# Mamba and mixture-of-experts kernel: the gate projection beside the first scan, one product for B, C and step size, and the last two blocks as routing groups of their own

## The chip, the cores and the metric

One core of a Trainium2 chip runs the whole kernel. The metric is device time in microseconds for one execution, the median of several. The engines run side by side and meet only at semaphores: TensorE (PE) multiplies and transposes, VectorE (DVE) and ScalarE (ACT) do elementwise work and can read TensorE's result banks, GpSimd (POOL) does elementwise work in the main memory of the core and issues indirect DMAs, and SyncE (SP) issues the plain DMAs.

## What is computed

Eight sequences of 1024 tokens with 512 channels pass through two residual layers:

```
n   = layernorm(x)
u,z = n @ in_proj.T                       # 512 and 512 channels
xc  = silu(causal_conv4(u) + conv_b)
B,C,s = xc @ x_proj.T                     # 16, 16 and 1 values for each token
dt  = softplus(s)
h[d,n] = exp(dt*A[d,n]) * h[d,n] + dt*B[n]*xc[d]     # along the tokens
y   = (sum_n h[d,n]*C[n] + D*xc) * silu(z)
x1  = x + y @ out_proj.T
m   = layernorm(x1)
top 2 of 8 experts by m @ router.T + b, weights w1, w2 (normalised)
out = x1 + w1 * (m @ W_e1) + w2 * (m @ W_e2)
```

All of it is in fp32, so each matrix product of the program shows as two matmul instructions.

## The kernel before

The tokens are cut into 16 blocks of 512; two blocks make a sequence. The program is one list of numbered iterations j from -1 to 20 (`iteration`), and each engine walks the same list of steps in the same order and executes those that are its own. Iteration j works on several blocks at once:

- the scan of block j: 64 places (16 states n, four channel groups c). At each place ACT computes a decay (L694) into one of two banks, DVE scans (L817), POOL computes the inputs `u` of two channel groups at a time (L560), PE transposes the states (`h_T`, L997) into one of two banks, and DVE adds them up over the states with weight C (`h_sum`, L829 and L832). `LAG` and `HT` set how many places behind the scan this happens. With LAG = 0 the first of four transposes is issued one place ahead of its sum, the others two places ahead.
- PREP of block j+1: load x, layernorm, transpose, in-projection (`project` 0 to 7, of which 4 to 7 are the gate z), convolution, `silu_x`, `c_project` (B and C by token, 32 matmuls with 32 columns), `dt_project` (8 matmuls with 512 columns), `b_project` (B transposed back), `dt_exp`, `dt_plus`, `b_scale`, `b_store`; the rows of B come back by DMA as `b_ring`. `silu_z` closes the gate.
- POST of block j-1: `y_T`, `y_skip`, `y_gate` (POOL), `out_project`, residual, layernorm, router, top 2, weights, `rank`, and the scatter of the weighted rows to the experts' regions in HBM (two indirect DMAs for each 128 tokens).
- EXPERTS: a routed group (one sequence, 24 tiles of 128 rows) is worked off in two iterations of 12 tiles, two iterations after its post: `rows_load`, four transposes, an eviction, 8 matmuls, an eviction and a store. `new_sequence` computes the group's table on DVE in odd iterations; it waits until the stores of the tiles before are done.
- COMBINE of block j-5: `fetch` of x1, two accumulating indirect gathers for each 128 tokens, `store`.

Where a side step stands among the 64 places is written out by hand in tables (`POST`, `PREP`, `EXPERTS`, `COMBINE`). Side work takes one of four result banks (`WORK`). A step that waits blocks everything behind it on its engine, and SP's loads and stores are such steps as well.

Scans run in iterations 0 to 15. Iteration 16 has the last four sums, the post of block 15 and 12 tiles; 17 and 18 have 12 tiles each (`closing_steps`, with two buffers for the rows), and combine goes on until iteration 20. At the start all weights are loaded on SP's queue ahead of x (L428 to L436), and every engine waits for all of them before its first step.

## Time and profile before

| | |
|---|---|
| median of 3 runs | 3035.31 us (3031.69 to 3042.91) |
| profiled execution, its time | 3033.59 us |
| its span, first to last instruction | 3031.7 us |
| PE busy | 2435.8 us, 80% |
| DVE busy | 2314.1 us, 76% |
| ACT busy | 1435.6 us, 47% |
| POOL busy | 1810.3 us, 60% |
| mean granted clock of TensorE | 0.887 of full speed |

### The profile page before, as it was taken

The page shows a single profiled execution, that of the slowest core. Times are in us where ns is not written, and L with a number is a line of the kernel's source. Part 1 is how long each engine was busy: PE and PEld are TensorE (multiplying, and loading weights), DVE is VectorE, ACT ScalarE, POOL GpSimd, SP SyncE. Part 2 cuts the span into 40 slices and gives each one's busy share as a digit, 9 for nine tenths or more (in the row PEclk, how much of TensorE's full clock was granted, in tenths as well). Part 3 has the DMA queues.
Part 4 walks back from the last instruction along what each step waited for, and adds up shares of the span by engine and source line. Part 5 has one row for each costly group of instructions (what it writes and reads, how often), then busy time and mean ns, then how long its engine had stood idle before and what let it go on. Part 6 is the DMA issues. An engine that isn't in the chain of part 4 may idle for free.

```text
span 3031.7 us, 35667 instructions
## 1 busy us (share of the span) xinstructions
PE 2435.8 (80%) x10000; PEld 1466.7 (48%) x10000; DVE 2314.1 (76%) x3233; ACT 1435.6 (47%) x2386; POOL 1810.3 (60%) x1418
## 2 busy tenths in 40 slices
PE   5677777798979899798979898797979898778770
PEld 3344444454545555455545554554545454544330
DVE  1788998988888888888888887888888888881000
ACT  2453546354555546354545546464545555342220
POOL 0555666556566757567676767577666767572223
PEclk9777777799989999898979999899989899888895
DMA  1773432223234434334334444344334444343665
GB/s 58 260 253 102 140 125 80 87 81 114 77 102 115 129 112 129 108 115 132 108 112 119 126 122 131 110 117 131 107 114 121 129 115 126 105 144 110 175 173 109
DMA packets 195502, 373.16 MB, mean 123 GB/s; under 512 B 23024, under 2 KB 23024, under 8 KB 195312
## 3 DMA queue, kind: packets, MB, share of 16 engines
q1 hardware_dynamic: 146576, 263.91, 27.1%
q0 software_dynamic: 28672, 67.13, 10.5%
q10 hardware_dynamic: 20064, 39.85, 3.6%
q8 instruction: 87, 1.43, 0.2%
q14 instruction: 103, 0.84, 0.1%
HBM read 212.99 MB, written 157.81 MB: 122 GB/s over the span
## 4 chain that ended last, share of the span: by engine, by line
PE 38%; DVE 19%; issue 16%; POOL 11%; ACT 9%; DMA 5%; SPq 1%; DVEq 0%; POOLq 0%; ACTq 0%
PE work L992 28%; DVE h L817 7%; POOL u L560 6%; PE hT L997 6%; DVE acc L832 6%; ACT decay L694 2%; DVE xc L850 2%; PE work L997 2%; DMA x_out<-result_scratch,rows_of 2%; POOL x_out L661 1%; PE work L1046 1%; ACT L694 1%; POOL row_scratch L645 1%; POOL row_scratch L647 1%; ACT xc L730 1%
## 5 line engine op out<-in xcount | busy, mean ns | idle before, releaser
L560 POOL TENSOR_TENSOR u<-xc,b_ring 128x1024 f32<-128x1024 f32 x512 | 1230.8, 2416 | 778.8 <-DVE h L817 424.2
L694 ACT ACTIVATE decay<-dt,neg_a 128x512 f32<-128x512 f32 x1024 | 699.7, 689 | 680.4 <-DVE h L817 671.3
L997 PE MATMUL hT<-ident,h 128*128 128x128 f32 x4096 | 680.7, 305 | 320.9 <-DVE acc L832 173.4
L997 PEld LDWEIGHTS hT<-ident,h 128*128 128x128 f32 x4096 | 530.4, 157 | 573.6 <-DVE acc L832 246.9
L832 DVE SCALAR_TENSOR_TENSOR acc<-hT,ct,acc 128x512 f32<-128x512 f32 x960 | 700.2, 730 | 134.1 <-PE hT L997 132.5
L992 PE MATMUL work<-w_exp,xeT 128*128 x1536 | 721.1, 614 | 34.1 <-ACT xeT L784 15.5
L817 DVE TENSOR_TENSOR_SCAN h<-decay,h_last,u 128x512 f32<-128x512 f32 x512 | 653.0, 1275 | 90.7 <-ACT decay L694 66.7
L817 DVE TENSOR_TENSOR_SCAN h<-decay,u 128x512 f32<-128x512 f32 x512 | 621.5, 1214 | 106.6 <-ACT decay L694 92.3
L992 PE MATMUL work<-xnT,w_in 128*128 128x512 f32 x1024 | 469.2, 602 | 0.8 <-ACT xnT L709 0.8
L992 PEld LDWEIGHTS work<-w_exp,xeT 128*128 128x128 f32 x1536 | 286.7, 195 | 361.8 <-issue 360.5
L661 POOL DMA_INDIRECT x_out<-result_scratch,rows_of x128 | 205.8, 1608 | 189.6 <-DMA x_out<-x_scratch 100.2
L992 PEld LDWEIGHTS work<-xnT,w_in 128*128 128x128 f32 x1024 | 188.4, 194 | 192.9 <-issue 192.9
L992 PE MATMUL work<-w_out,sz 128*128 128x512 f32 x512 | 256.1, 648 | 4.7 <-POOL sz L582 4.7
L792 ACT ACTIVATE ye<-work 128x512 f32<-128x512 f32 x180 | 106.0, 589 | 241.2 <-PE work L992 223.0
L784 ACT ACTIVATE xeT<-work 128x512 f32<-128x512 f32 x192 | 112.7, 588 | 130.6 <-PE work L997 127.4
L992 PEld LDWEIGHTS work<-w_out,sz 128*128 128x128 f32 x512 | 103.1, 212 | 114.0 <-issue 114.0
L850 DVE SCALAR_TENSOR_TENSOR xc<-work,w_conv,xc 128x511 f32<-128x511 f32 (+2 forms) x192 | 142.2, 741 | 17.7 <-ACT edge L717 16.3
L997 PE MATMUL work<-ident,xe 128*128 128x128 f32 x720 | 112.0, 279 | 41.2 <-DMA xe<-row_scratch 41.1
L582 POOL TENSOR_TENSOR sz<-xc,sz 128x512 f32<-128x512 f32 x64 | 79.8, 1269 | 85.8 <-DVEq L876 85.8
L997 PEld LDWEIGHTS work<-ident,xe 128*128 128x128 f32 x720 | 86.4, 145 | 55.1 <-issue 54.8
L702 ACT ACTIVATE xn<-xn,shift,rstd 128x512 f32<-128x512 f32 x64 | 51.3, 807 | 120.2 <-POOL shift L550 120.2
L992 PE MATMUL work<-w_xp,xc 128*128 128x32 f32 x512 | 74.2, 305 | 23.9 <-ACT xc L730 23.9
(140 smaller groups left out, 1892.5 us busy)
## 6 DMA issues: line engine op xcount, KB each, us to landing
b_ring<-b_scratch SPq DMA_DIRECT2D x256, 256.0 KB, 3.9
xe<-row_scratch SPq DMA_DIRECT2D x180, 256.0 KB
result_scratch<-ye SPq DMA_DIRECT2D x180, 256.0 KB
row_scratch<-x_out ACTq DMA_DIRECT2D x32, 1024.0 KB, 5.0
xn<-in_x SPq DMA_DIRECT2D x64, 256.0 KB, 4.6
x<-in_x SPq DMA_DIRECT2D x64, 256.0 KB, 4.3
x_scratch<-x SPq DMA_DIRECT2D x64, 256.0 KB, 4.4
x_out<-x_scratch SPq DMA_DIRECT2D x64, 256.0 KB, 3.3
```

The source lines that it names most:

```text
L560: nc.gpsimd.tensor_tensor(out=u[:, at:at + 2, :], in0=xc[:, half, 2 * k:2 * k + 2, :], in1=b_ring[:, n % ROWS:n % ROWS + 1, :].to_broadcas ...
L582: nc.gpsimd.tensor_tensor(out=sz[:, 1 - half, c, :], in0=xc[:, 1 - half, c, :], in1=sz[:, 1 - half, c, :], op=ALU.mult).then_inc(y_gated, 1)
L661: nc.gpsimd.indirect_dma_start(x_out[:, q % 2, :], None, res_dram[:, :], bass.IndirectOffsetOnAxis(ap=rows_of[(pair - 3 + half) % 3][:, at ...
L694: nc.scalar.activation(decay_bank[g % 2][:], dt[:, half, :], ACT.Exp, scale=neg_a[:, c, n:n + 1]).then_inc(decay_ready, 1)
L702: nc.scalar.activation(xn[:, q % 2, :], xn[:, q % 2, :], ACT.Identity, bias=shift1[:, q:q + 1], scale=rstd[:, q:q + 1]).then_inc(xn_ready, 1)
L784: nc.scalar.activation(xeT[:, i % 2], ps[:].rearrange("p (k t) -> p k t", k=C), ACT.Copy).then_inc(free, 1)
L792: nc.scalar.activation(ye_of(j, i), ps[:], ACT.Copy).then_inc(free, 1)
L817: nc.vector.tensor_tensor_scan(out=h[:, n % 2, c, :], data0=decay_bank[g % 2][:], data1=u[:, g % UR, :], initial=first, op0=ALU.mult, op1= ...
L832: nc.vector.scalar_tensor_tensor(out=acc[:, q, :], in0=hT_bank[k % HT][:], scalar=ct[:, ip, q, m:m + 1], in1=acc[:, q, :], op0=ALU.mult, o ...
L850: nc.vector.scalar_tensor_tensor(out=xc[:, 1 - half, c, away:T], in0=ps[:, 0:T - away], scalar=w_conv[:, c, EDGE - away:TAPS - away], in1= ...
L992: last = nc.tensor.matmul(ps, left(k), right(k), start=(k == 0), stop=(k == C - 1))
L997: last = nc.tensor.transpose(ps[:, k * P:(k + 1) * P], tile(k), ident[:])
```

## The change

- **Start.** SP loads the four x tiles of block 0 first (the third and fourth into `x1`), then the first half of `w_in`, then the rest; seven small weights are issued by ACT. Each engine waits only for what its next step needs.
- **Gate.** `project` 4 to 7 become `z_project`. In every iteration from 0 on they stay in the same iteration; those of block 0 move from iteration -1 into the first places of iteration 0, with their evictions and `silu_z`.
- **B, C and step size.** One `xp_project` (8 matmuls with 512 columns, 33 rows of result) takes the place of `c_project`; `xp_evict` (ACT) copies its 33 rows into `dt`; `dt_project` becomes 2 matmuls that pick the row of the step size and spread it over 128 rows; `c_T` transposes C (4 transposes), with one eviction; B is scaled straight from the result bank.
- **Lag.** LAG is 1: sums and transposes run one place later, and every transpose is issued two places ahead of its sum.
- **Groups.** Blocks 0 to 13 make seven groups of two with 23 tiles each; blocks 14 and 15 are groups of their own with 15 tiles each. Tiles of a group run as 12 and 11 in iterations 3 to 14; the seventh group's 23 all run in iteration 15; the two last groups' 15 in iterations 16 and 17. Combine takes two blocks in iteration 15 and two in 16, one in 17 and one in 18; the last block is gathered into `x1`, whose x1 rows are fetched ahead. From iteration 15 on the tiles alternate between two buffers. The table of a group (`new_group`) has two copies. Zeroing of the result buffer is gone.
- All places in the tables are new.

```diff
-    XT = TOP * SQ + E
-    LAG = 0
+    GROUPS = [(b, 2) for b in range(0, BLOCKS - 2, 2)] + [(BLOCKS - 2, 1), (BLOCKS - 1, 1)]
+    TILES = [TOP * Q * n + E - 1 for first, n in GROUPS]
+    for g in range(len(GROUPS) - 3):
+        EXPERT_PLAN[2 * g + 3] = (g, 0, XT - XT // 2)
+        EXPERT_PLAN[2 * g + 4] = (g, XT - XT // 2, XT // 2)
+    for i in range(3):
+        g = len(GROUPS) - 3 + i
+        EXPERT_PLAN[BLOCKS - 1 + i] = (g, 0, TILES[g])
+    COMBINE_PLAN = {j: [j - 5] for j in range(5, BLOCKS - 1)}
+    COMBINE_PLAN[BLOCKS - 1] = [BLOCKS - 6, BLOCKS - 5]
+    COMBINE_PLAN[BLOCKS] = [BLOCKS - 4, BLOCKS - 3]
+    COMBINE_PLAN[BLOCKS + 1] = [BLOCKS - 2]
+    COMBINE_PLAN[BLOCKS + 2] = [BLOCKS - 1]
+    LAG = 1
...
-        "c_project": [34.97, 38.72],
-        "dt_project": [40.54],
-        "dt_exp": [44.54],
-        "b_project": [44.57],
-        "b_store": [55.2],
+        "dt_project": [38.23],
+        "dt_exp": [41.7],
+        "xp_project": [37.25],
+        "xp_evict": [40.85],
+        "c_T": [40.72],
+        "b_store": [45.82],
...
+    FIRST_GATE = [(0.2 + 2 * c, ("z_project", c, 0)) for c in range(C)] + [(1.6 + 2 * c, ("z_evict", c, 0)) for c in range(C)] + [(9, ("silu_z", 0, 0))]
...
+        if j == BLOCKS + 2:
+            return ([("gather", q, 0) for q in range(Q)] + [("gather", q, 1) for q in range(Q)] + [("store", q) for q in range(Q)])
...
+        rows = [[("fetch", q), ("gather", q, 0), ("gather", q, 1), ("store", q)] for q in range(Q)] + [[("fetch_last", q) for q in range(Q)]]
+        steps = [("new_group", 0)]
+        for i, tile in enumerate(tiles):
+            steps += tile
+            steps += rows[i // 3] if i % 3 == 0 and i // 3 < len(rows) else []
...
+            for q in range(Q):
+                sync.dma_start(xn_of(0, q), x[q * P:(q + 1) * P, :]).then_inc(first_loaded[q], 16)
+            sync.dma_start(w_in[:, :, 0:D], in_w[:, 0:D].rearrange("(k p) n -> p k n", p=P)).then_inc(project_loaded, 16)
+            sync.dma_start(w_in[:, :, D:2 * D], in_w[:, D:2 * D].rearrange("(k p) n -> p k n", p=P)).then_inc(weights_loaded, 16)
...
+                    elif s[0] == "xp_evict":
+                        bank_no, before = use_of(j, ("xp_project", 0))
+                        act.wait_ge(work_full[bank_no], before + 1)
+                        nc.scalar.activation(dt[0:XP, 1 - half, :], work_bank[bank_no][0:XP, :], ACT.Copy).then_inc(xp_ready, 1)
...
+                        product(ps[0:XP, :], lambda k: w_xp[:, k, :], lambda k: xc[:, 1 - half, k, :]).then_inc(full, 1)
                     elif s[0] == "dt_project":
                         ps, full = take(j, s)
-                        pe.wait_ge(xc_ready, (p + 1) * C)
-                        product(ps[:], lambda k: w_xp[:, k, 2 * N:2 * N + 1].to_broadcast([P, P]),
-                                lambda k: xc[:, 1 - half, k, :]).then_inc(full, 1)
+                        pe.wait_ge(xp_ready, p + 1)
+                        nc.tensor.matmul(ps[:], pick_dt[0:XP, :], dt[0:XP, 1 - half, :], start=True, stop=True).then_inc(full, 1)
```

## Rows read from the trace of the kernel before

**Rows 1.** The span in 40 slices: busy tenths of DVE, and TensorE's granted clock.
```profile
DVE  1788998988888888888888887888888888881000
PEclk9777777799989999898979999899989899888895
```

**Rows 2.** Stages: us; busy PE, PEld, DVE, ACT, POOL; clock; DMA; GB/s.
```profile
86.50:227.30 140.80, 95.00 (x368) 62.58 (x369) 124.96 (x147) 68.99 (x115) 77.24 (x45) 0.71 0.75 261
227.30:385.30 158.00, 116.86 (x481) 76.76 (x480) 143.72 (x193) 77.66 (x121) 99.47 (x78) 0.77 0.37 123
...
1554.20:1725.70 171.50, 147.12 (x624) 88.33 (x624) 148.66 (x211) 88.44 (x144) 112.86 (x85) 0.92 0.40 117
1725.70:1891.10 165.40, 146.31 (x626) 88.59 (x626) 140.57 (x194) 89.79 (x156) 113.73 (x90) 0.94 0.42 122
...
2563.50:2718.10 154.60, 116.56 (x487) 73.62 (x488) 135.35 (x189) 64.35 (x103) 105.34 (x76) 0.84 0.41 120
2718.10:2838.60 120.50, 86.80 (x269) 43.33 (x268) 20.83 (x66) 24.56 (x42) 34.61 (x45) 0.87 0.45 129
2838.60:2889.80 51.20, 49.91 (x144) 23.89 (x144) 0.00 (x0) 12.90 (x24) 10.85 (x8) 0.95 0.70 184
2889.80:2954.30 64.50, 50.02 (x144) 24.16 (x144) 0.00 (x0) 13.69 (x25) 13.73 (x9) 0.91 0.66 171
2954.30:3031.70 77.40, 0.00 (x0) 0.00 (x0) 0.00 (x0) 0.00 (x0) 24.59 (x16) 0.50 0.54 112
```

**Rows 3.** Timeline, first 87 us: start, duration, engine, line, operation, idle before.
```profile
9.06 13.78 SPq L447 DMA_DIRECT2D xn<-in_x  x4
...
15.84 0.69 DVE L837 BATCH_NORM_STATS2 stat<-xn 128x6 f32<-128x512 f32 x1 [14.44 <-DMA xn<-in_x]
...
31.79 17.01 PE L992 MATMUL work<-xnT,w_in 128*128 128x512 f32 x32 [0.78 <-ACT xnT L709]
...
53.52 7.03 PE L992 MATMUL work<-w_xp,xc 128*128 128x32 f32 x32 [4.71 <-ACT xc L730]
...
60.36 6.09 PE L992 MATMUL work<-xc,w_xp 128*128 128x512 f32 x8
...
66.49 0.60 ACT L737 ACTIVATE sp<-work 128x512 f32<-128x512 f32 x1 [5.62 <-PE work L992]
...
74.50 0.34 SPq L461 DMA_DIRECT2D b_scratch<-sp  x1
...
79.62 4.65 POOL L560 TENSOR_TENSOR u<-xc,b_ring 128x1024 f32<-128x1024 f32 x2 [51.48 <-DMA b_ring<-b_scratch]
...
86.51 4.57 DVE L817 TENSOR_TENSOR_SCAN h<-decay,u 128x512 f32<-128x512 f32 x4 [12.04 <-ACT decay L694]
```

**Rows 4.** Timeline, iteration 10 at `c_project`: start, duration, engine, line, operation, idle before.
```profile
1833.58 1.87 PE L992 MATMUL work<-w_xp,xc 128*128 128x32 f32 x16
...
1837.26 3.60 PE L992 MATMUL work<-xc,w_xp 128*128 128x512 f32 x8
```

**Rows 5.** Groups by line, whole span: count | busy, mean ns | idle before.
```profile
L832 DVE SCALAR_TENSOR_TENSOR acc<-hT,ct,acc 128x512 f32<-128x512 f32 x960 | 700.2, 730 | 134.1 <-PE hT L997 132.5
```

**Rows 6.** Timeline, the end: start, duration, engine, line, operation, idle before.
```profile
2832.26 0.35 DVE L959 TENSOR_TENSOR table_row<-tiles_to,tile_no 1x192 f32<-1x192 f32 x1 [43.52 <-DMA result_scratch<-ye]
...
3002.27 1.54 POOL L661 DMA_INDIRECT x_out<-result_scratch,rows_of  x1 [0.30 <-issue]
...
3007.59 1.54 POOL L661 DMA_INDIRECT x_out<-result_scratch,rows_of  x1 [3.79 <-DMA x_out<-result_scratch,rows_of]
...
3012.65 0.34 SPq L503 DMA_DIRECT2D out<-x_out  x1
...
3016.40 0.32 SPq L498 DMA_DIRECT2D x_out<-x_scratch  x1
3019.23 1.54 POOL L661 DMA_INDIRECT x_out<-result_scratch,rows_of  x1 [1.71 <-DMA x_out<-x_scratch]
...
3024.30 1.54 POOL L661 DMA_INDIRECT x_out<-result_scratch,rows_of  x1 [3.54 <-DMA x_out<-result_scratch,rows_of]
```

613 lines of the change are left out of this document (337 added, 276 removed).

## The prediction, made before the changed kernel ran

> **What bounds the kernel now.** I read the span in slices first [rows 1]: DVE is busy 80 to 90% of each slice for nine tenths of the span, idle in the first slice but for a tenth, and idle again in the last three. So there are three stages: a start, a long loop, and an end. Then I cut the span at the first scan of each iteration [rows 2]. The first scan starts at 86.5 us. A full iteration takes 165.4 us (even j) or 171.5 us (odd j, with the table of a group); DVE is busy 140.6 to 148.7 us of it, 85 to 87%, PE 146 to 147 us, 86 to 88%. Two engines are near full together, and the 23 to 25 us in which DVE is idle are mutual waits of in-order queues. The last scan ends at 2718.1 us, and 313.6 us follow that hold 21 us of DVE work: 120.5 us with post of block 15 and 12 tiles, then 24 tiles, then 77.4 us in which PE does nothing and only gathers run. The clock is 0.92 to 0.94 in the full loop and 0.71 to 0.77 in its first two iterations.
>
> Of the waits in the loop, I read the groups by line [rows 5]: DVE waits 134.1 us before `h_sum` for transposes, 8.4 us an iteration. Going through the instances of the twelve full iterations, about half of it, 4.0 us, stands before the first of each four sums: the one that the schedule gives a lead of one place only.
>
> **The change part by part.** The sum is made against the profiled execution, 3033.6 us, which is 1.7 us under the median of the runs shown.
>
> *Start.* x is issued at 9.06 us behind 3 MB of weights and DVE's first statistics begin at 15.84; the second pair comes later still, and the first product starts at 31.79 [rows 3]. With x ahead of all, the first statistics can start at about 5.2 us (issue at 0.7, and some 4.5 us to land, the median of x loads in the list of DMA issues). The chain from there to the second eviction took 7.3 us, and a second pair that no longer waits adds some 3.5 us: first product at 16 us, 15.8 us earlier. The first half of `w_in` is there by then: 3.1 MB landed in 14.3 us, so x and that half, 2 MB, need some 9 us. ACT's seven DMA issues take the 7 us that SP needed for them and end at about 8 us, ahead of its first `norm_apply`.
> The Trainium skill, "DMA: Bandwidth & Descriptors", section "Issuing engines are not separate DMA queues", says that DMAs issued from several engines interleave on the same 16 DMA engines and save only issue time. By that rule the small weights and `w_out` could hold the first half of `w_in` back until all 4.2 MB are there, and the sum would be worse by up to 3 us. No run here shows it yet.
>
> Behind the convolution nothing changes until `silu_x` ends at 53.5. Then `c_project` takes 7.03 us and `dt_project` 6.09, so `dt_exp` starts 13.0 us later, at 66.49 [rows 3]. New: 8 matmuls (3.4 us, or 6.8 at half clock), a copy of 0.6, two matmuls (0.9 to 1.7) and some 0.5 of semaphores, 5.4 to 9.6 us; I take 7.5, a gain of 5.5. From `dt_exp` to `b_store` it is 8.0 us before, because B's transposes stand behind 16 gate matmuls; without that 6.0. From `b_store` to the end of the first `u` it is 7.5 us and stays so, but the first scan began at 86.51 only, 4.5 us after that `u`, since ACT was still at `silu_z`; that goes. In all the first scan comes 28 us earlier (20 to 30).
>
> *The gate of block 0* now lies beside the first scan: 32 matmuls, 13.8 us at full clock and 27 at half, four evictions and a `silu_z` of 4.5 us with its table loads. Half of the matmuls can run in the gap of some 13 us in which DVE waits for B to come back; the rest stands between the transposes of an iteration whose clock is 0.71 [rows 2]. DVE pays 8 us (2 to 18).
>
> *The loop, B, C and step size.* At full clock 16 matmuls of `c_project` take 1.97 or 1.87 us and the 8 of `dt_project` 3.60 [rows 4]. Removed: 3.8 + 3.6 us. Added: 3.6 for `xp_project`, 0.9 for two matmuls, and transposes for transposes. PE has 2.9 us less. ACT swaps four copies of 0.19 us for one of 0.6 and one of 0.2. The added wait: `dt_project` at place 38 waits for `xp_evict` at place 40 on ACT, and `h_T` is queued behind it on PE. ACT gets there after the decay of place 40, which needs scan 38. From the end of scan 38 that is 0.7 + 0.6 us, the two matmuls 0.9, and the transposes 0.7 with 0.5 for semaphores, 3.4 us; DVE has three scans and two sums to do before it needs them, 5.5 us. So the lag covers it; under LAG = 0 it would cost some. I take it as nothing, and 2 us an iteration if the cover is gone.
>
> *Lag.* Every transpose gets two places of lead, 3.7 us, so the 4.0 us before the first sums go. What is late next is the product that stands ahead of a transpose (3.6 us), and that remains. At the border of two iterations `y_T` now waits for a sum that is one place later, and its 16 transposes stand ahead of the next sum: +1.2 us.
> Together with 1.5 us for the shorter PE queue I take -4.3 us in each of twelve full iterations, -52 us. The bounds are wide, since every place in the tables is new: -90 (all of the 8.4 us of waits for transposes goes, net of the border) and +15.
>
> *Iteration 15* gets 11 tiles more. A tile is 4.16 us of PE (49.91 us for 12 tiles, rows 2, third row from the end), so PE goes from 116.6 to 162.4 us. At the share that full iterations reach (88%) that is 183 us, with PE alone as the bound 165; I take 180, as DVE has 5 to 13 us less to do there than in a full iteration. Against 154.6: +25 us (8 to 40). The eight added gathers cost POOL 13 us, hidden if first and second gather of a pair have a `u` between them.
>
> *Iteration 16* has 15 tiles instead of 12 and combines two blocks. Before, it took 120.5 us to the first transposes of the next stage, the last part of it because the table waited 43.5 us for the last store (released at 2832.26) [rows 6]; the two copies end that. Now POOL is late: a block's gathers in the free-running end take 38.7 us (77.4 for two), so 77 for two, 22 for its other work (34.6 less 8 gathers of 1.6) and 14 until the first: 113, and SP's last store behind it. I take 122, +2 us (-12 to +20).
>
> *Iteration 17.* Before, 24 tiles from 2838.6 to the last product at 2949.6, 111 us. Now 15 tiles. In `closing_steps` SP has `fetch`, then `store` of the same rows right behind it, and waits there for both gathers: 2.8 us from fetch to gather, 5.3 to the second and 5.1 to the store [rows 6], 13.2 us in which neither a load nor a store of a tile is issued. Three more loads, of which one must land, and the third store take some 5 us, so 18.5 us for three tiles instead of 12.5. Four such groups and three tiles more make 86.5 us: -24.5 us. If SP didn't hold the tiles it would be 62, so -49.
>
> *After the last product*: 82 us before (block 14 and 15 one after the other). Now eight gathers that don't wait on each other, 1.84 us apart, 12.9 us to the last; 0.8 and 2.5 before them for eviction and store, then 5.1 and 2.3 to the end as in the last rows: 24, with some reserve 26. -56 us.
>
> Sum: -28 + 8 - 52 + 25 + 2 - 24.5 - 56 = -125.5. 3033.6 - 125.5 = 2908, and 2910 for the median.
>
> **The rivals.**
> - *The loop gains nothing.* The new places and the waits for `xp_evict` eat what the lag gives. For it: the tables are a whole, 8.4 us of waits are only a third of DVE's idle time, and most of the rest is ACT's (decays behind `silu_x`, `dt_exp` and `silu_z`), which isn't touched. Loop 0 to +10 us: 2965.
> - *The loop gains twice as much*, or SP doesn't hold the tiles in iteration 17: 2860 to 2885. For it: in iterations with fewer products the same DVE work runs with less idle time (158.0 us with 143.7 busy).
> - *The tiles moved forward cost what they save.* Iteration 15 at 195 us and iteration 16 at 140, bound by POOL, whose gathers stand ahead of `rank` weights and scatters: +33 us, 2943.
> - *Slower: the clock falls.* PE's work is 88% of an iteration at clock 0.93; with 117 us of work in 155 to 158 us the rows show 0.77 and 0.84 [rows 2]. Less work, in shorter pieces, could bring the lower level (1.2 GHz) back into the loop. Outside the full iterations the sum is -73.5 us, so they would have to be 6.1 us longer, 174.5 instead of 168.4 on average. At 88% that is PE at 153.6 us with 144 us of today's work: the clock falls below 0.93 x 144 / 153.6 = 0.87. At 0.84, the value of iteration 15, it would be 159 us of work, 181 us an iteration, +152 us: 3112. Against it: full iterations have a quarter more PE work than those, and lose 2%.
> - *The change doesn't do what it says* at the end: the table or the scatters hold iteration 17 anyway. That is within the 140 us of the third rival.
>
> **How the numbers follow.** Forecast 0.50, loop without gain 0.18, loop with twice the gain or a free SP queue 0.15, moved tiles costly 0.12, clock 0.05. A measurement of this kernel can tell about 0.5%, 15 us, from no change. Within it lies part of the second case with a bad end (0.02), above it nearly all of the clock's case (0.03), so 0.95 faster, 0.02 same, 0.03 slower. The range leaves out the clock's case and the outer parts of the bounds: the uncertain terms (loop +-35, iteration 15 +-15, 16 +-16, 17 +-20, gate +-8) combine to some 45 us. 2855 to 2975.
>
> **What would show it.** Right: first scan near 58 us; full iterations at 161 to 167 us with the idle time of `h_sum` at half; iteration 15 near 180; about 86 us of tiles in iteration 17 with gaps of PE before each third load, SP's `store` ahead of it; no more than 27 us after the last product. Wrong: full iterations as long as before, with waits for transposes behind `dt_project`; iteration 15 above 195; a clock under 0.87 in the loop; a first scan after 66 us.

## The result, and the profile after

The changed kernel takes 3014.7 us (median of 7 runs, 3004.9 to 3021.8) against 3036.3 us of the kernel before on the same chip: ratio 0.9931, 95% interval 0.9912 to 0.9950. It is faster, by 0.7% instead of the 4% predicted. Its profiled execution took 3012.2 us, of which 3010.4 are the span. The span in slices, busy tenths of DVE and granted clock, as in [rows 1]:

```profile
DVE  3889898898888888888888888888888888765100
PEclk8678777798979999798979899898979898899977
```

DVE is busy from the first slice on, and the idle slices at the end are fewer; between them the two pictures are nearly the same. The stages of [rows 2], cut in the same way (us; busy PE, PEld, DVE, ACT, POOL; clock; DMA; GB/s): iterations 0, 1, 9, 10, 15, then 16, the tiles of 17, and what follows the last product.

```profile
59.20:215.70 156.50, 103.52 (x351) 57.85 (x352) 125.29 (x146) 74.72 (x118) 79.42 (x46) 0.71 0.69 240
215.70:376.30 160.60, 118.82 (x450) 71.00 (x450) 143.11 (x191) 78.12 (x118) 99.17 (x78) 0.74 0.37 118
...
1539.60:1713.60 174.00, 147.90 (x598) 86.67 (x598) 148.58 (x212) 89.72 (x142) 114.40 (x86) 0.89 0.39 116
1713.60:1877.30 163.70, 142.02 (x581) 84.15 (x582) 140.79 (x194) 90.15 (x152) 111.80 (x90) 0.90 0.42 119
2549.60:2739.70 190.10, 157.09 (x618) 91.72 (x619) 136.47 (x190) 74.44 (x123) 118.03 (x83) 0.89 0.52 146
2739.70:2872.10 132.40, 95.25 (x316) 49.01 (x315) 28.28 (x88) 28.68 (x50) 48.55 (x54) 0.89 0.63 167
2872.10:2985.30 113.20, 70.10 (x180) 33.05 (x180) 0.00 (x0) 16.34 (x29) 12.31 (x8) 0.79 0.43 111
2985.30:3010.40 25.10, 0.00 (x0) 0.00 (x0) 0.00 (x0) 0.60 (x1) 12.30 (x8) 0.57 0.70 136
```

DVE's work in a full iteration is what it was (148.6 and 140.8 us); the length hardly moved. From the first scans of each iteration, in the two profiled executions:

| stage | before | after | difference | predicted |
|---|---|---|---|---|
| to the first scan | 86.5 | 59.2 | -27.3 | -28 |
| iteration 0 | 140.8 | 156.5 | +15.7 | +8 |
| iterations 1 and 2 | 313.7 | 320.9 | +7.2 | 0 |
| iterations 3 to 14 | 2022.4 | 2013.0 | -9.4 | -52 |
| iteration 15 | 154.6 | 190.2 | +35.6 | +25 |
| iteration 16, to the next transposes | 120.5 | 132.4 | +11.9 | +2 |
| iteration 17, tiles | 111 | 113.2 | +2.2 | -24.5 |
| after the last product | 82 | 25.1 | -57 | -56 |

The start and the end went as worked out. Timeline of the start, to hold against [rows 3] (start, duration, engine, line, operation, idle before):

```profile
4.10 0.69 DVE L925 BATCH_NORM_STATS2 stat<-xn 128x6 f32<-128x512 f32 x1 [2.71 <-DMA xn<-in_x]
...
16.07 15.50 PE L1084 MATMUL work<-xnT,w_in 128*128 128x512 f32 x32 [0.73 <-issue]
...
36.37 5.21 PE L1084 MATMUL work<-xc,w_xp 128*33 128x512 f32 x8 [4.80 <-ACT xc L819]
...
49.55 0.34 SPq L533 DMA_DIRECT2D b_scratch<-sp  x1
...
56.80 4.64 POOL L639 TENSOR_TENSOR u<-xc,b_ring 128x1024 f32<-128x1024 f32 x2 [46.85 <-DMA b_ring<-b_scratch]
59.25 2.34 DVE L902 TENSOR_TENSOR_SCAN h<-decay,u 128x512 f32<-128x512 f32 x2 [9.72 <-POOL u L639]
```

The first product starts at 16.07 us (16 predicted), right behind the last eviction of `xnT` (it ended at 15.97). The first half of `w_in` had landed at 10.36 us, and `w_out` landed at 14.68: what the prediction drew from the Trainium skill, "DMA: Bandwidth & Descriptors", section "Issuing engines are not separate DMA queues", that the other transfers could hold `w_in` back, cost nothing here.

In the loop, DVE's groups in iteration 10 (count | busy us, mean ns | idle before, and what ended it), first the kernel before, then the changed one:

```profile
L817 DVE TENSOR_TENSOR_SCAN h<-decay,u 128x512 f32<-128x512 f32 x64 | 77.7, 1215 | 12.9 <-ACT decay L694 10.1 <-POOL u L560 2.2 <-PE hT L997 0.3
L832 DVE SCALAR_TENSOR_TENSOR acc<-hT,ct,acc 128x512 f32<-128x512 f32 x60 | 43.8, 729 | 9.8 <-PE hT L997 9.8
...
L881 DVE TENSOR_TENSOR x<-work,x 128x512 f32<-128x512 f32 x4 | 2.7, 682 | 0.2 <-PE work L992 0.2
```

```profile
L902 DVE TENSOR_TENSOR_SCAN h<-decay,u 128x512 f32<-128x512 f32 x64 | 77.7, 1215 | 12.6 <-ACT decay L776 11.4 <-DVE xc L966 0.9
L917 DVE SCALAR_TENSOR_TENSOR acc<-hT,ct,acc 128x512 f32<-128x512 f32 x60 | 43.8, 730 | 6.0 <-PE hT L1089 5.8
...
L914 DVE TENSOR_SCALAR acc<-hT,ct 128x512 f32<-128x512 f32 x4 | 2.9, 732 | 1.0 <-PE work L1143 1.0
L974 DVE TENSOR_TENSOR x<-work,x 128x512 f32<-128x512 f32 x4 | 2.7, 686 | 3.7 <-PE work L1084 3.7
```

In this iteration the wait of the sums for transposes fell by 4.0 us, the amount predicted for the lag. Over the whole span it fell from the 134.1 us of [rows 5] to 99.3, which is 2.2 us an iteration, half of that. And a wait of 3.7 us stands at the third `residual`, for a `w_out` product that has an expert product ahead of it on PE.

### The profile page after: what moved, and what is told of

Its sections match the earlier page's. It is cut to its first block, busy times and chain, and to the rows that moved or that the text cites. A ratio compares the mean times of both kernels' runs of the same rounds, so it can differ in the third digit from the quotient of the medians.

```text
span 3010.4 us, 34543 instructions
## 1 busy us (share of the span) xinstructions
PE 2434.5 (81%) x9510; PEld 1410.5 (47%) x9510; DVE 2322.5 (77%) x3253; ACT 1452.1 (48%) x2353; POOL 1809.7 (60%) x1420
## 3 DMA queue, kind: packets, MB, share of 16 engines
q1 hardware_dynamic: 144272, 263.26, 27.3%
## 4 chain that ended last, share of the span: by engine, by line
PE 47%; DVE 22%; issue 13%; DMA 6%; ACT 6%; POOL 5%; DVEq 0%; SPq 0%; POOLq 0%; ACTq 0%
PE work L1084 34%; DVE h L902 9%; PE hT L1089 7%; DVE acc L917 7%; PE work L1089 3%; POOL u L639 3%; DMA x_out<-result_scratch,rows_of 2%; PE work L1143 2%; DVE xc L940 2%; DMA b_ring<-b_scratch 1%; ACT decay L776 1%; DVE xc L966 1%; DVE acc L914 1%; DMA xe<-row_scratch 1%; DMA result_scratch<-ye 1%
## 5 line engine op out<-in xcount | busy, mean ns | idle before, releaser
L1089 PE MATMUL hT<-ident,h 128*128 128x128 f32 x4096 | 702.4, 308 | 389.3 <-DVE acc L917 277.4
L1084 PE MATMUL work<-w_exp,xeT 128*128 x1528 | 751.3, 638 | 40.4 <-DVE dt L952 13.8
L917 DVE SCALAR_TENSOR_TENSOR acc<-hT,ct,acc 128x512 f32<-128x512 f32 x960 | 700.4, 730 | 99.3 <-PE hT L1089 96.9
L1084 PE MATMUL work<-xnT,w_in 128*128 128x512 f32 x1024 | 484.1, 618 | 2.2 <-DVE dt L952 1.5
L1084 PEld LDWEIGHTS work<-w_exp,xeT 128*128 128x128 f32 x1528 | 296.3, 204 | 370.2 <-issue 369.3
L743 POOL DMA_INDIRECT x_out<-result_scratch,rows_of x120 | 192.6, 1605 | 185.0 <-DMA x_out<-x_scratch 95.8
L1084 PEld LDWEIGHTS work<-xnT,w_in 128*128 128x128 f32 x1024 | 194.8, 200 | 203.4 <-issue 201.0
L1084 PE MATMUL work<-w_out,sz 128*128 128x512 f32 x512 | 240.4, 614 | 0.0
L878 ACT ACTIVATE ye<-work 128x512 f32<-128x512 f32 x165 | 96.7, 586 | 127.8 <-PE work L1084 109.5
L940 DVE SCALAR_TENSOR_TENSOR xc<-work,w_conv,xc 128x511 f32<-128x511 f32 (+2 forms) x192 | 141.0, 742 | 18.6 <-ACT edge L805 17.2
L1089 PE MATMUL work<-ident,xn 128*128 128x128 f32 x352 | 68.0, 337 | 42.1 <-DMA xn<-row_scratch 30.2
L974 DVE TENSOR_TENSOR x<-work,x 128x512 f32<-128x512 f32 x64 | 43.8, 685 | 70.7 <-PE work L1084 70.6
```

What stands on the lines that cost most here:

```text
L743: nc.gpsimd.indirect_dma_start(row, None, res_dram[g % 2][:, :], bass.IndirectOffsetOnAxis(ap=rows_of[g % 3][:, pos * Q + q, k:k + 1], axi ...
L878: nc.scalar.activation(ye_of(tile), ps[:], ACT.Copy).then_inc(free, 1)
L917: nc.vector.scalar_tensor_tensor(out=acc[:, q, :], in0=hT_bank[k % HT][:], scalar=ct[:, ip, q, m:m + 1], in1=acc[:, q, :], op0=ALU.mult, o ...
L940: nc.vector.scalar_tensor_tensor(out=xc[:, 1 - half, c, away:T], in0=ps[:, 0:T - away], scalar=w_conv[:, c, EDGE - away:TAPS - away], in1= ...
L1084: last = nc.tensor.matmul(ps, left(k), right(k), start=(k == 0), stop=(k == C - 1))
L1089: last = nc.tensor.transpose(ps[:, k * P:(k + 1) * P], tile(k), ident[:])
```

## The experiments

Each ratio is against the kernel before, run on the same chip (its medians lie between 3034.0 and 3040.1 us). Times of stages come from each kernel's one profiled execution. How far they can be trusted shows in five kernels whose instructions in iterations 3 to 14 are the same (the changed one, e1, e4, e5, e10): 2013.0, 2022.7, 2019.4, 2019.2 and 2019.1 us, mean 2018.7. So the changed kernel's own profile was a quick one: by the mean its loop gained 4 us rather than 9. Two single profiles of this stretch can differ by 10 us with nothing changed, so neither gain can be told from none. Iteration 0 took 153.6 to 156.7 us in the six kernels that leave it as it is (the changed one, e1, e5, e8, e9, e10), iteration 15 took 190.2 to 193.4 us in the six that leave that one (the changed one, e1, e4, e8, e9, e11).

**e1_store_late: what holds iteration 17.**

```diff
-rows = [[fetch q, gather q 0, gather q 1, store q] for q] + [[fetch_last ...]]
+rows = [[fetch q, gather q 0, gather q 1, store q-1] for q] + [[store Q-1, fetch_last ...]]
```

> The changed kernel, but in iteration 17 each store of an output block row (it waits for that row's two gathers) is issued three tiles later on SyncE, behind the next row's fetch, as in the kernel before. My theory: the fifteen tiles took 113.2 us because SyncE stood 13 us per row at the store, with the loads of the next tiles behind it, and the third tile's product, its store and the next fetch behind those. Then the stretch from iteration 17's first transposes to the end of its last product falls from 113.2 to about 62 us (15 tiles at about 4.1 us, no hold), the other stretches stay, and the profiled execution falls from 3012 to about 2962 us. Rival: the gathers or the loads themselves set the pace (they are queued behind each other on the DMA engines), and the stretch stays within 5 us of 113. Between them: about 85 us if the store still holds SyncE for some us because a row's gathers take longer than three tiles.

2972.2 us (2968.8 to 2978.0), ratio 0.9788 (0.9764 to 0.9812): 42 us under the changed kernel. SyncE's issues in iteration 17 (start, duration), in the changed kernel:

```profile
2899.85 0.37 SPq L565 DMA_DIRECT2D x_out<-x_scratch  x1
2912.86 0.34 SPq L577 DMA_DIRECT2D out<-x_out  x1
2913.95 0.35 SPq L555 DMA_DIRECT2D xe<-row_scratch  x1
...
2924.16 0.37 SPq L565 DMA_DIRECT2D x_out<-x_scratch  x1
2937.08 0.34 SPq L577 DMA_DIRECT2D out<-x_out  x1
```

PE waits meanwhile for the load that stands behind the store:

```profile
2916.99 1.09 PE L1089 MATMUL work<-ident,xe 128*128 128x128 f32 x4 [10.47 <-DMA xe<-row_scratch]
```

e1:

```profile
2901.06 0.37 SPq L566 DMA_DIRECT2D x_out<-x_scratch  x1
2902.26 0.34 SPq L578 DMA_DIRECT2D out<-x_out  x1
2903.35 0.35 SPq L556 DMA_DIRECT2D xe<-row_scratch  x1
...
2912.66 0.43 SPq L566 DMA_DIRECT2D x_out<-x_scratch  x1
```

From a fetch to the next it is 24.3 us with the store behind its own fetch and 11.6 us without. The stretch of the tiles as one row of stages:

```profile
2885.70:2950.20 64.50, 60.41 (x180) 29.47 (x180) 0.00 (x0) 16.05 (x29) 12.31 (x8) 0.97 0.72 194
```

64.5 us instead of 113.2 (62 expected), and the granted clock rises from 0.79 to 0.97. The theory holds; the rival (gathers or loads set the pace) is out. The whole gained 42 us and not 49: this execution's other stretches were longer, the loop by 9.7 us, which is within what repeats of it differ by.

**e4_gate_evict_later: iteration 0.**

```diff
-[(1.6 + 2 * c, ("z_evict", c, 0)) for c in range(C)] + [(9, ("silu_z", 0, 0))]
+[(3.6 + 2 * c, ("z_evict", c, 0)) for c in range(C)] + [(10.95, ("silu_z", 0, 0))]
```

> The changed kernel with block 0's four gate evictions of iteration 0 two places later on ScalarE (places 3.6 to 9.6 instead of 1.6 to 7.6; the silu behind them at 10.95). My theory: in iteration 0 VectorE waited 16.9 us for decays because ScalarE stood at these evictions for products that were queued on TensorE behind the transposes of h; with the evictions behind the products this wait falls by some 10 us, iteration 0 from 156.5 to about 146 us, and the time to about 3004 us. Rival: TensorE's gate products themselves hold the transposes of h, and with them the sums and scans; then the wait moves from the decays to the sums and iteration 0 stays within 2 us of 156.5 (3012 to 3017 us).

Iteration 0 took 146.9 us instead of 156.5 (153.6 to 156.7 in the kernels that leave it). ScalarE's wait at these evictions, in the changed kernel and in e4 (groups, up to 100 us; the fourth eviction of the changed kernel lies later):

```profile
L813 ACT ACTIVATE sz<-work 128x512 f32<-128x512 f32 x3 | 1.8, 590 | 12.4 <-PE work L1084 12.4
```

```profile
L813 ACT ACTIVATE sz<-work 128x512 f32<-128x512 f32 x4 | 2.4, 588 | 2.5 <-PE work L1084 2.5
```

The mechanism is shown: 7 to 10 us of iteration 0. In the whole the time is 3012.6 us, ratio 0.9926 (0.9903 to 0.9949), which can't be told from the changed kernel's.

**e2_expert_behind: the wait at the residual.**

```diff
-"expert": [11.51, 14.24, ...   "expert_evict": [14.04, 16.16, ...
+"expert": [11.51, 14.95, ...   "expert_evict": [14.04, 17.1, ...
-"norm_T": [..., 15.03, 15.85]  "rows_T": [9.09, 12.41, 17.23, ...
+"norm_T": [..., 15.03, 16.9]   "rows_T": [9.09, 12.41, 17.65, ...
```

> The changed kernel with one order changed in the loop: the second expert product of an iteration stands on TensorE behind the third w_out product instead of ahead of it (its eviction and store one place later, the fourth norm transposes and the third row transposes one place later to leave a bank free). My theory: the 3.6 us per iteration that VectorE waits at the third residual for that w_out product is what ate the 4.0 us that the later sums gave; with the product ahead the wait goes, iterations 3 to 14 fall by 3 to 4 us each (2013 to about 1970 us) and the time from 3014.7 to about 2972 us. Rival: the wait is only the place at which VectorE meets a TensorE and ScalarE that are late anyway; it comes back at the decay activations (ScalarE stands at the expert eviction) or at the next transposes, and the loop gives under 1 us per iteration (3003 to 3017 us).

3048.0 us, ratio 1.0033 (1.0015 to 1.0051); iterations 3 to 14 took 2050.8 us, 32 more. In iteration 10:

```profile
L902 DVE TENSOR_TENSOR_SCAN h<-decay,u 128x512 f32<-128x512 f32 x64 | 77.7, 1214 | 16.2 <-ACT decay L776 11.5 <-POOL u L639 3.5 <-DVE xc L966 1.0
...
L974 DVE TENSOR_TENSOR x<-work,x 128x512 f32<-128x512 f32 x4 | 2.7, 682 | 0.3 <-PE work L1084 0.3
```

The wait at the residual is gone, 3.4 us, and 3.6 us more stand before the scans. My theory falls. The rival has the mechanism, but it was too kind: it had 3003 to 3017 us.

**e3_lag0 and e6_before_lag1: the lag, with the new places and with the old.**

```diff
-    LAG = 1        (e3, in the changed kernel)
+    LAG = 0
-    LAG = 0        (e6, in the kernel before)
+    LAG = 1
-        "y_skip": [3.86, 3.99, 3.99, 7.24],
+        "y_skip": [4.86, 4.99, 4.99, 7.24],
```

> The changed kernel with LAG back at 0: every sum of the scan and the transposes behind it stand one place earlier, as in the kernel before; nothing else. My theory: the later sums are worth the 4.0 us per iteration by which the wait of the sums for their transposes fell, so the loop of iterations 3 to 14 is 12 x 4 = 48 us longer than in the changed kernel, iterations 0 to 2 about 9 us and iterations 15 about 4, and the time is 3014.7 + 60 = about 3075 us. Rival: VectorE's waits pass into each other, since the decays, the residuals and the transposes all hang on how far VectorE is ahead; then the loop changes by under 1 us per iteration and the time is 3005 to 3030 us.

> The kernel before with one part of the change alone: LAG is 1, so that every sum of the scan and the transposes behind it stand one place later; the first three skip products stand one place later with them (4.86 to 4.99), since the last sum now lies at place 4. With LAG taken away, iterations 3 to 14 of the changed kernel took 2071 us, with it 2013 us, while those of the kernel before, without it, took 2022.5 us. Theory A: the lag is worth 4.8 us per iteration by itself, and what else changed in the loop (the new places of the steps, the new products) costs 4 us per iteration; then iterations 3 to 14 fall here from 2022.5 to 1960 to 1975 us and the time from 3036 to 2975 to 2990 us. Theory B: the lag pays only with the new places, which were chosen for it; then the loop stays within 10 us of 2022.5 and the time within 3025 to 3045 us.

e3 3056.6 us, ratio 1.0070 (1.0048 to 1.0093); e6 3138.8 us, ratio 1.0333 (1.0306 to 1.0359). Iterations 3 to 14:

| | LAG 0 | LAG 1 |
|---|---|---|
| places and products of before | 2022.4 | 2107.5 |
| places and products of the change | 2071.3 | 2013.0 |

With the new places the lag is worth 53 to 58 us (against the mean or the profile), as e3's first theory had it (48). But it costs 5 to 8 us of iteration 0, 4.5 of 1 and 2, and 3 to 6 of 15, where that theory had gains; so e3 is 42 us slower in all and not 60. With the old places it costs 85 us. e6 in iteration 10, to hold against the rows of before above:

```profile
L817 DVE TENSOR_TENSOR_SCAN h<-decay,u 128x512 f32<-128x512 f32 x64 | 77.8, 1215 | 24.9 <-ACT decay L694 17.2 <-PE hT L997 5.2 <-POOL u L560 1.5
L832 DVE SCALAR_TENSOR_TENSOR acc<-hT,ct,acc 128x512 f32<-128x512 f32 x60 | 43.6, 727 | 4.7 <-PE hT L997 4.7
```

The sums wait 5.1 us less in this iteration, and the scans 12 us more. Both of e6's theories were too kind. The rest of the change costs 49 us of the loop at LAG 0 and saves 89 to 95 at LAG 1, so the expectation's step from e3, that it costs 4 us per iteration by itself, falls: neither factor has a price of its own.

**e7_places_before: the old places for the first 30 places, all else changed.**

```diff
-"y_T": [3.07, 3.23, 3.41, 3.49],  "out_project": [10.01, 13.55, 14.89, 16.47],
+"y_T": [2.37, 2.7, 2.72, 3.95],   "out_project": [8.64, 12.09, 13.95, 15.69],
...                                (and so on for every step of the first 30 places)
```

> The changed kernel with, in iterations up to 14, the places of the kernel before for the steps of the first 30 places: the tail of the block before (y, gate, w_out products, residuals, second norm, router), the norm, the x half of the projection and its taps, and the first four expert tiles; LAG, the products for B, C and step size, the gate's places and all else stay as changed. Theory A: the new places are what costs 4 us per iteration (they crowd three w_out products, two expert products, two router products and seven sets of transposes between places 13.5 and 19.7 of TensorE, where the iteration was 5.5 us slower than before); then iterations 3 to 14 fall from 2013 to some 1965 to 1980 us and the time from 3014.7 to 2970 to 2985 us. Theory B: the cost lies in the new products and their waits, or in the clock; then the loop stays within 10 us of 2013, the time within 3005 to 3025 us. Theory C: the two sets of places do not fit at their border near place 30, or the old ones lack the lag, and the loop is 10 us or more slower.

3227.4 us, ratio 1.0625 (1.0597 to 1.0652), iterations 3 to 14 2208.4 us. Theory C: in iteration 10 DVE waits 8.0 us at the convolution's taps for ScalarE, where it waited for nothing in the changed kernel, and 21.2 us before the scans instead of 12.6. A half of one plan and a half of the other don't fit.

**e5_thin_products and e8_thin_loop: is it PE's work?**

```diff
+if j == BLOCKS - 1 and s[1] >= EXPERT_PLAN[j][2] // 2:      (e8: if j < BLOCKS - 1)
+    matmul(ps, xeT[:, tile % 2, 0, :], w_exp[expert, 0:D], start=True, stop=True)
+    continue
```

> The changed kernel with part of the computation left out: in iteration 15 the expert products of the last 12 of the 23 tiles take one matmul of 128x128 by 128x512 instead of four (so these tiles' results are not the reference's); their loads, transposes, evictions, stores and all waits stay. Iteration 15 took 190.2 us against 163.7 us for iteration 14. Theory A: the twelve added tiles cost by TensorE's work (PE 157 us busy of 190); 12 x 2.6 us = 31 us of it goes, and iteration 15 falls by 18 to 30 us. Theory B: they cost by the waits that their evictions put on ScalarE ahead of the decays (VectorE waited 33 us for decays), which are there whatever a product takes; then iteration 15 falls by less than 8 us.

> The changed kernel with part of the computation left out: in iterations 3 to 14 every expert product takes one matmul of 128x128 by 128x512 instead of four; loads, transposes, evictions, stores and all waits stay. It takes 2.6 us from each of 11 or 12 products, some 30 us of TensorE's work per iteration. In the changed kernel TensorE was busy 48.1 us of the 48.5 us that places 12 to 28 took in iteration 10, but 18.4 of 28.8 us at places 0 to 12. Theory A: the loop is bound by TensorE's queue in those full stretches, so the waits of VectorE for residuals, decays and sums are all its echo; three expert products lie in them (7.8 us), and an iteration falls by 8 to 15 us, the loop by 100 to 180 us. Theory B: VectorE's order with ScalarE sets the pace (as the twelve thin products of iteration 15 suggest, where 15 us less TensorE work brought 5 us), and an iteration falls by less than 4 us, the loop by under 50 us.

Both leave part of the computation out and have one run. e5: 3010.9 us; iteration 15 took 184.9 us, 5 to 9 less than in the kernels that leave it, with PE busy 142.3 us instead of 157.1. e8: 2975.6 us; iterations 3 to 14 took 1969.8 us, 43 to 49 less, 4 us per iteration. Theory B in both, at its edge. Iteration 10 of e8:

```profile
1686.50:1849.90 163.40, 125.32 (x518) 74.79 (x517) 139.85 (x194) 90.23 (x152) 112.92 (x91) 0.83 0.42 121
```

66 matmul instructions less in 11 tiles (28.6 us at 2.6 us a tile) shorten PE's time by 16.7 us only, at a clock of 0.83 instead of 0.90, and the iteration is as long as in the changed kernel (163.7 us). The odd one before it went from 174.0 to 167.8. The waits that hang on PE did shrink: on the mean of iterations 3 to 14 those at the residuals by 3.6 us, those of the sums by 1.6, and those of the scans for ScalarE from 8.2 to 4.7. In their place the scans wait 4.9 us for POOL's `u` instead of 0.7, half of it at place 38, where in iteration 10 POOL worked on the router's weights until 1785.99 us ahead of that `u` (the scan waited 3.54 us). So what e8 shows is that PE's work is not the only limit of a full iteration, not that it is none.

**e9_tiles_early and e10_late_spaced: the same work at other places.**

```diff
+EXPERTS_EVEN: "rows_T": [1.8, 7.6, ...], "expert": [5.7, 8.8, ...], "expert_evict": [7.3, 10.4, ...]   (e9)
-"late_rows_evict": [..., 33.48, 37.05, 39.93, ...]  "late_expert_evict": [..., 36.93, 43.19, ...]      (e10)
+"late_rows_evict": [..., 33.23, 35.78, 38.33, ...]  "late_expert_evict": [..., 36.13, 38.68, ...]
```

> The changed kernel with, in the even iterations from 4 to 14, the first two expert tiles moved out of the crowded stretch of TensorE to where it idled: row transposes from places 9.1 and 12.4 to 1.8 and 7.6, products from 11.5 and 14.2 to 5.7 and 8.8, evictions, stores and loads with them. Their routing table is there since the iteration before. Theory A: TensorE's queue at places 12 to 20 is what VectorE waits for; 7 us of work leave it, and the waits there (2.2 us at places 12 to 16, 5.2 at 16 to 20 in iteration 10) mostly go: an even iteration falls by 4 to 7 us, the six of them by 25 to 40 us. Theory B: as in the run that only swapped two products, the waits come back elsewhere (at places 4 to 12, where ScalarE would now stand at the moved evictions), and an even iteration changes by less than 2 us or grows.

> The changed kernel with the last 13 of the 23 expert tiles of iteration 15 spaced evenly, 2.55 places apart, and with each eviction of the row transposes two places behind them and of the product 2.5 places behind it. In the changed kernel ScalarE stood 46.3 us of iteration 15 at evictions of row transposes, some of them 0.3 to 1.7 places behind. Theory A: iteration 15 is slow because ScalarE stands at evictions ahead of decays (VectorE waited 33 us for decays); then it falls by 8 to 15 us from 190.2. Theory B: TensorE's amount of work between transposes of h sets it; the same work evenly spread gives less than 4 us.

e9: 3019.6 us, ratio 0.9936 (0.9916 to 0.9956), iterations 3 to 14 2016.2 us, which is the changed kernel's. On the mean of the even iterations 6 to 14, places 12 to 20 are 5.2 us shorter, as theory A had it, and places 0 to 12 are 5.9 us longer: theory B. e10: 3027.2 us, ratio 0.9969 (0.9950 to 0.9987); iteration 15 took 201.3 us, 8 to 11 more. There the sums wait 2.5 us instead of 12.5 and the scans 55.7 instead of 32.8. Neither theory foresaw that.

**e12 to e15: more decays ready ahead of the scans.**

```diff
+DECAYS = 4          (e12; e14 and e15: 3)
-decay_bank = [bank(f"decay{i}") for i in range(2)]
+decay_bank = [bank(f"decay{i}") for i in range(2)] + [sb(f"decay_sb{i}", [P, T]) for i in range(DECAYS - 2)]
+AHEAD = 2           (e13; e14 and e15: 1): decay g + AHEAD issued ahead of scan g
```

> The changed kernel with four decay buffers instead of two (two in PSUM, two in SBUF), the order of ScalarE's instructions unchanged. To make room, the weights of the last expert are left out and its tiles use those of the one before, so part of the result is not the reference's; the instructions are as many as before. Theory A: ScalarE's holds at evictions reach VectorE because only two decays can lie ready; with four, the waits for decays (7 to 12 us of an iteration) fall by half or more and iterations 3 to 14 fall by 3 to 6 us each (2013 to 1945 to 1975 us). Theory B: ScalarE cannot run ahead at all, since each eviction stands in its order at about the place at which TensorE, held to VectorE's pace by the transposes of h, makes its product; then four buffers bring under 1.5 us per iteration. Theory C: scans whose decay lies in SBUF take longer than the 1.22 us with PSUM, and the loop is slower.

> As e12 (four decay buffers, the last expert's weights left out), and the decays also stand two places earlier in ScalarE's order, ahead of the evictions of those places. Theory A: the order was what passed ScalarE's holds on; the waits for decays nearly go (under 3 us of an iteration), iterations 3 to 14 fall by 6 to 10 us each (to 1895 to 1940 us), iteration 15 by 10 to 20 us (it waited 33 us for decays), the whole to 2860 to 2920 us. Theory B: VectorE then waits at the sums for the transposes of h instead, because TensorE has no slack (busy 142 to 148 us of 164 to 172); the loop falls by under 3 us per iteration.

> The changed kernel with three decay buffers and the decays one place earlier in ScalarE's order, the whole computation kept: the third buffer has its place in SBUF because the routing table's scratch row shares the memory of sp (with one wait on VectorE before a table and one on ScalarE before the step-size activations, both long met). Theory A, the order of the decays: a bit more than half of what two places give, 3 to 6 us per iteration, and the time from 3014.7 to 2940 to 2975 us. Theory B (TensorE has no slack): 3000 to 3015 us.

> e14 with the stores of iteration 17 three tiles later and block 0's gate evictions two places later. By the sum of what each gives (-42, -2 to -9, and e14's -40 to -75 by theory A) the time is 2890 to 2930 us; by theory B about 2960 to 2970 us.

3260.1 and 3238.6 us (one run each), 3172.4 us (ratio 1.0460, 1.0432 to 1.0488) and 3121.0 us (1.0280, 1.0258 to 1.0302): theory C of e12, and far above what the others had. e13, iteration 9:

```profile
L905 DVE TENSOR_TENSOR_SCAN h<-decay_sb,h_last,u 128x512 f32<-128x512 f32 x32 | 62.1, 1939 | 4.0 <-POOL u L642 3.5 <-DVE xc L969 0.4
...
L905 DVE TENSOR_TENSOR_SCAN h<-decay,h_last,u 128x512 f32<-128x512 f32 x32 | 40.7, 1272 | 0.7 <-DVE xc L969 0.5 <-ACT decay L779 0.2
...
L977 DVE TENSOR_TENSOR x<-work,x 128x512 f32<-128x512 f32 x4 | 2.7, 684 | 4.7 <-PE work L1087 4.7
```

Scans wait 0.2 us for ScalarE, where iteration 9 of the changed kernel has 7.4. But a scan whose decay lies in SBUF takes 1939 ns on average instead of 1272. One of them, with POOL beside it:

```profile
1723.64 3.01 DVE L905 TENSOR_TENSOR_SCAN h<-decay_sb,h_last,u 128x512 f32<-128x512 f32 x1
...
1728.75 1.27 DVE L905 TENSOR_TENSOR_SCAN h<-decay_sb,h_last,u 128x512 f32<-128x512 f32 x1
```

```profile
1723.22 2.35 POOL L642 TENSOR_TENSOR u<-xc,b_ring 128x1024 f32<-128x1024 f32 x1 [4.44 <-DVE h L905]
1728.92 1.11 POOL L673 TENSOR_SCALAR veps<-mv 128x2 f32<-128x2 f32 x1 [3.35 <-DVE mv L982]
```

The scan at 1723.64 lies on the `u` that runs until 1725.57 and ends 1.1 us behind it, as if it had begun then; the next one, with no `u` beside it, takes 1.27 us. It is so throughout: of the 210 scans from SBUF that began while a `u` ran, 201 ended 1.05 to 1.12 us behind the end of that `u`. Over the span, 393 scans from SBUF that overlap an instruction of POOL took 2.12 us on average and 119 that don't 1.24; with the decay in PSUM it is 1.24 us either way (414 and 98). What buffers and order give by themselves can't be read from these times.

**e16_decay_order and e17_order_and_ends: the order alone, both buffers in PSUM.**

```diff
+FROM_PE = ("rows_evict", "expert_evict", "z_evict", "norm_evict", "norm2_evict")
+if names & set(FROM_PE) and not names & set(FOR_OTHERS):
+    steps.append(("decay", (at + 1) // C, (at + 1) % C))
 steps += place[at]
```

> The changed kernel, the whole computation and its two decay buffers in PSUM kept; in each place of ScalarE's order that holds an eviction of a TensorE product (row transposes, expert products, gate products, transposes of the norms) and nothing on which VectorE or TensorE would stand at an earlier place, the decay of the next place is issued ahead of these evictions. Theory A: VectorE's waits for decays come from ScalarE standing at such evictions with the next decay behind them; then these waits halve (7 to 12 us of an iteration, 33 us in iteration 15), iterations 3 to 14 fall by 3 to 5 us each, iteration 15 by 8 to 15 us, and the time is 2945 to 2970 us. Theory B: the evictions now wait for a scan more, TensorE's banks come free later, and the wait turns into one for sums or residuals: the time is within 3000 to 3025 us.

> e16 with the stores of iteration 17 three tiles later and block 0's gate evictions two places later. By theory A 2900 to 2930 us, by theory B 2955 to 2980 us (the two late edits alone give about 2967 us).

e16 3040.3 us, ratio 1.0011 (0.9997 to 1.0024); e17 2996.4 us, ratio 0.9875 (0.9860 to 0.9891). Iteration 15 of the changed kernel, then of e16:

```profile
L902 DVE TENSOR_TENSOR_SCAN h<-decay,h_last,u 128x512 f32<-128x512 f32 x64 | 81.7, 1277 | 32.8 <-ACT decay L776 20.2 <-PE hT L1089 6.2 <-POOL u L639 5.0
L917 DVE SCALAR_TENSOR_TENSOR acc<-hT,ct,acc 128x512 f32<-128x512 f32 x60 | 43.8, 731 | 12.5 <-PE hT L1089 12.4
```

```profile
L909 DVE TENSOR_TENSOR_SCAN h<-decay,h_last,u 128x512 f32<-128x512 f32 x64 | 81.7, 1276 | 19.1 <-PE hT L1096 6.8 <-POOL u L646 6.6 <-ACT decay L783 4.7
L924 DVE SCALAR_TENSOR_TENSOR acc<-hT,ct,acc 128x512 f32<-128x512 f32 x60 | 43.9, 732 | 28.4 <-PE hT L1096 26.2 <-issue 2.2
```

Waits for ScalarE fall from 20.2 to 4.7 us, those for transposes rise from 18.6 to 33.0, and the iteration takes 196.9 us, where it took 190.2 to 193.4 in the kernels that leave it as it is. Iterations 3 to 14 took 2037.4 us, 19 more than the mean. Theory B, and worse than it said. e17 lies above the range of theory B too (2955 to 2980): it has the edits of e1 and e4 besides the order, and is 0.9% slower than e1 by the two ratios.

**e11_combined: the edits of e1, e4 and e9 together.**

> The changed kernel with three edits at once: the stores of iteration 17 three tiles later, block 0's gate evictions two places later, and the first two tiles of the even iterations early. If each holds what it gave or should give alone (-42, -2 to -9, -25 to -40 us) the time is 2920 to 2945 us; if the early tiles give nothing, about 2965 us; over 2975 us would mean that they cost.

2969.1 us (2960.6 to 2971.6), ratio 0.9766 (0.9743 to 0.9789): 2.3% faster than the kernel before and, by the two ratios, 1.7% faster than the changed one; it can't be told from e1, whose edit brings nearly all of it.

## Why the prediction was wrong

The direction was right; the time was 105 us above the forecast and above the range. By its steps:

- **Start: right.** -27.3 for -28, the first product, `xp_project` and `b_store` where they were placed.
- **After the last product: right.** 25.1 us for 26, gathers 1.84 us apart.
- **The gate of block 0: term too small,** +15.7 for +8. I had listed the four evictions but priced PE's products alone. The evictions stand on ScalarE ahead of decays and wait for products that are queued behind transposes of h. e4 moves them and gets 7 to 10 us back. The lag, which I had given no price here, takes 5 to 8 us of this iteration too (e3).
- **Iterations 1 and 2: left out,** +7.2. With the lag taken away they are 4.5 us shorter (e3), so the lag explains most of it: in the two together it takes 2.6 us from the waits of the sums and adds 7.5 us to those of the scans.
- **The loop: the failed step,** -4 to -9 for -52. The term was made of the waits that the lag takes from the sums, less 1.2 us at the border, and 1.5 us for the shorter PE queue. Two things failed in it: the step from a wait that goes to time that goes, and the price of nothing for the new places of all other steps. DVE's idle time in an iteration, mean of iterations 3 to 14, by what it stands before (us):

| | length | scans | sums | residuals | all else |
|---|---|---|---|---|---|
| before | 168.5 | 12.9 | 8.8 | 0.1 | 2.0 |
| changed | 167.7 | 10.2 | 6.6 | 3.6 | 2.7 |
| e3: the change without the lag | 172.6 | 6.8 | 18.1 | 0.0 | 3.2 |
| e6: the lag alone | 175.6 | 21.4 | 6.4 | 0.1 | 2.0 |
| e2: residual's wait taken away | 170.9 | 15.2 | 7.7 | 0.2 | 3.3 |
| e16: decays ahead of evictions | 169.8 | 9.1 | 8.0 | 4.7 | 3.4 |

The 4.0 us before the first of four sums are there in the kernel before, as read. But without the lag the rest of the change makes them 15.9 us and the iteration 4.1 us longer (e3). The lag takes most of that away again, 11.5 us of the sums' waits, of which the scans and the residuals get 7.0 back: 4.4 to 4.9 us an iteration, about what I had given it, but on a wait that the new places had made. In the kernel before it takes 2.4 us from the sums and adds 8.5 to the scans (e6). In the other runs that took a wait of DVE away it came back as well: e2: 3.4 us away, 5.0 back before the scans alone; e9: 5.2 away, 5.9 back between places; in iteration 15, e10: 10 away, 23 back, and e16. The traces say where the new places cost: places 16 to 20 took 10.1 us in the kernel before and 15.5 in the changed one, 15.6 in e3. Between scans 14 and 20 PE now has 37 matmuls of `w_out` and expert products where it had 29. Places 36 to 48, with the new products for B, C and the step size, took 31.3 us and take 31.0. No run has places and products apart, since e7's mixture didn't fit.

The rival "the loop gains nothing" was the right one for this stage, and I gave it 0.18. Of its reasons the new places hold; `xp_evict` has no visible part, since the wait on PE at `dt_project` is 0.2 us in iterations 9 and 10 together. But that rival's time, 2965 us, is 50 us short as well: the other stages are 62 us above the forecast together. The gate, the loop and iterations 15 and 16 lie within the bounds that I had given them, iteration 17 doesn't. The range took the loop as +-35 where its stated bound reached 67 us above the term, and added the terms as if their errors would offset each other; all that were off were off to the same side.
- **Iteration 15: term too small,** +35.6 for +25, inside its bounds. I took PE's share as the measure; e5 takes 15 us of PE work away and gets 5 to 9 back. That the waits between the three engines grow with each tile fits, but is only argued.
- **Iteration 16: term too small,** +12 for +2. No experiment was made on it. In the timeline POOL issues gathers and scatters by turns from 2822 us on, the last gather at 2862.91, as the third rival says, but for less. That row's store holds SyncE until 2867.97, the next tile's load is issued at 2869.35 behind it, and PE has stood idle for 14.05 us when it starts at 2872.06. It is the same order of store and load as in iteration 17, but e1 leaves it as it is; the cause stays argued.
- **Iteration 17: right mechanism, wrong size,** +2 for -24.5. The hold was there, 13.0 us from fetch to store as worked out. But I let the third tile go on in the meantime. Its product stands on PE behind the transposes of the next tile, whose load is held (10.47 us of idle time on PE); so its store is late as well, and the next fetch is queued behind that store. A round is 13.0 us of hold and 11.3 us for three tiles one after the other, 24.3 instead of 18.5. With the store moved, it is 65 us, near the 62 that the prediction gave for a free SyncE (e1).
- **The clock:** that rival had the direction. It fell from 0.92 and 0.94 to 0.89 and 0.90 in full iterations, not below the 0.87 from which that rival was to decide.

What stays open is what sets the length of a full iteration. It isn't PE's amount of work alone: 18 us less of it gave 4 us, with the clock at 0.83 and a new wait for POOL (e8). Nor is it one wait (e2, e9, e16). DVE is busy 85 to 86% of it; that the rest belongs to the loop of waits between DVE, ScalarE, TensorE and, in e8, POOL as a whole agrees with all runs, but no run of the whole computation has a loop that is clearly shorter than the changed kernel's. A third decay buffer in PSUM wasn't tried: it would have to be taken from the four tiles of the work products, all of which the places use.

## What to carry to other kernels

In a loop of several in-order engines that are all 80 to 90% busy, don't add up the waits that an edit removes: ask what each engine does with the time, and don't count on any gain until a run shows it, with the order of steps that it will stand in: the lag by itself would have shown a loss (e6). A schedule of fixed places is one object: the same lag was worth -55 us with one set of places and +85 with another, and a mixture of two sets was worse than either. Gains that stood were those at a stage's edge, where one queue alone was late: x loaded first, gathers that don't wait on each other, and a store moved behind the loads that it held up, 42 us for one moved step.

## What the runs showed of the hardware

- A scan with both operands in SBUF that meets a running `u` of POOL waits until it has ended: 1.24 us without one beside it, 2.12 us on average with one, up to 4.43; with one operand in PSUM 1.24 us in both cases (e13). The Trainium skill, "SBUF — State Buffer", section "SBUF: two separate sides", says that VectorE with two SBUF inputs and GpSimd hold one port pair as an exclusive lock, and that the one that comes second blocks fully. The trace agrees: the scan of 3.01 us lay 1.93 us on a `u` and ended 1.08 us behind it.
- Fewer matmuls don't shorten PE's time in proportion. With a clock of 0.83 instead of 0.90 the same iteration gave back some of what it lost (e8), and in iteration 17 the clock was 0.79 with holds and 0.97 without (e1).
- The same instructions in iterations 3 to 14 took 2013 to 2023 us in five kernels, so one profile of this loop tells 0.5% and no less.
